# Two attentions on TensorE, VectorE and ScalarE: a rotation placed one step later, and a transposed output placed in another PSUM bank

## The reference, cut to what matters

```python
q, k = rotate(norm(x) @ wq.T + bq), rotate(ctx @ wk.T + bk)   # 16 heads of 8; no biases in layer 3
v = ctx @ wv.T + bv
p = softmax(q @ k.T / sqrt(8))                        # per head, 64 x 64
x = x + tanh(gate) * ((p @ v) @ wo.T + bo)
```

## Time and profile before

| | |
|---|---|
| median of 3 runs | 589.69 us |
| the profiled execution's own time | 589.77 us |
| its span, first to last instruction | 588.0 us |
| TensorE busy | 559.3 us |
| VectorE busy | 441.0 us |
| ScalarE busy | 402.3 us |
| first attention, from its first scores to the projection of its second half | 128.8 to 167.8 us |
| second attention, from and to the same steps | 439.9 to 478.5 us |

### The profile page before, as it was taken

The page is one execution under the profiler, slowest core; times in us unless marked ns, Lnnn a source line. Parts: engine busy times, 40 slices in busy tenths (PEclk is TensorE's granted clock), DMA queues, the critical chain, the costliest instruction groups (busy, mean ns, idle before and its releaser), DMA issues.

```text
span 588.0 us, 8733 instructions
## 1 busy us (share of the span) xinstructions
PE 559.3 (95%) x3258; PEld 387.0 (66%) x3258; DVE 441.0 (75%) x692; ACT 402.3 (68%) x561; POOL 101.9 (17%) x69
## 2 busy tenths in 40 slices
PE   8999999898999999999996999999999999999997
PEld 5688787656767767765331346566546677888886
DVE  3377987868839799987889775766768828787786
ACT  3698899855856755426999865534504858888875
POOL 5400000000210000003999703200000310000000
PEclk8999999999999999999999899999999999999999
DMA  6118120300100369220000024506400100811100
GB/s 242 33 41 310 50 71 1 116 1 2 56 1 2 127 243 230 65 72 1 7 1 1 1 71 117 174 3 175 147 36 3 42 32 3 322 42 67 36 2 36
DMA packets 19342, 43.81 MB, mean 75 GB/s; under 512 B 2090, under 2 KB 7594, under 8 KB 19300
## 3 DMA queue, kind: packets, MB, share of 16 engines
q1 hardware_dynamic: 19300, 43.25, 22.7%
HBM read 42.55 MB, written 0.70 MB: 74 GB/s over the span
## 4 chain that ended last, share of the span: by engine, by line
PE 69%; DVE 15%; ACT 11%; issue 3%; POOL 1%; DVEq 0%; ACTq 0%; POOLq 0%
PE ps L820 36%; ACT work L1219 7%; PE ps L862 4%; PE ps L569 3%; PE ps L552 3%; DVE h_lo L1756 2%; PE ps L846 2%; PE ps L848 2%; PE ps L847 2%; PE ps L686 2%; PE ps L559 2%; PE ps L659 2%; PE ps L887 2%; PE ps L801 2%; DVE h_act L1729 2%
## 5 line engine op out<-in xcount | busy, mean ns | idle before, releaser
L1756 DVE TENSOR_TENSOR h_lo<-h_act,h_hi 128x512 fp32r<-128x512 f32 (+1 forms) x114 | 103.6, 913 | 39.7 <-ACT h_hi L1266 38.9
L820 PE MATMUL ps<-n_hi,w_hi 128*128 128x512 f32 x224 | 86.8, 422 | 2.4 <-DVE h_act L1729 1.2
L1266 ACT CAST h_hi<-h_act 128x1024 fp32r<-128x1024 f32 (+1 forms) x88 | 75.4, 857 | 14.6 <-PE ps L820 12.1
L820 PE MATMUL ps<-n_hi,w_lo 128*128 128x512 f32 x224 | 79.7, 391 | 0.0
L820 PE MATMUL ps<-n_lo,w_hi 128*128 128x512 f32 x224 | 79.6, 390 | 0.0
L1969 POOL TENSOR_TENSOR rstd<-var_eps,minus_half 128x4 f32<-128x4 f32 x16 | 17.2, 1075 | 312.1 <-DVE var_eps L1411 312.1
L1219 ACT ACTIVATE work<-work,p_rest 128x2048 f32<-128x2048 f32 x31 | 59.5, 2000 | 1.0 <-DVE work L1609 1.0
L1259 ACT ACTIVATE h_act<-ps 128x512 f32<-128x512 f32 x44 | 26.3, 598 | 45.6 <-PE ps L820 45.4
L820 PE MATMUL ps<-h_hi,w_hi 128*128 128x512 f32 x162 | 56.2, 395 | 0.1
L820 PE MATMUL ps<-h_hi,w_lo 128*128 128x512 f32 x162 | 55.3, 390 | 0.0
L820 PE MATMUL ps<-h_lo,w_hi 128*128 128x512 f32 x162 | 55.3, 390 | 0.0
(11 more groups left out here) (235 smaller groups left out, 1041.1 us busy)
## 6 DMA issues: line engine op xcount, KB each, us to landing
work<-g_rows SPq DMA_DIRECT2D x36, 512.0 KB, 5.8
w_f<-in_w SPq DMA_DIRECT2D x20, 512.0 KB, 3.7
w_f<-in_w SPq DMA_DIRECT2D x8, 384.0 KB, 3.2
work<-g_rows SPq DMA_DIRECT2D x8, 256.0 KB, 7.3
work<-g_rows SPq DMA_DIRECT2D x4, 384.0 KB, 7.2
diag<-in_w SPq DMA_DIRECT2D x2, 512.0 KB, 4.7
work<-in_w SPq DMA_DIRECT2D x2, 512.0 KB, 4.4
w_f<-in_w_rest SPq DMA_DIRECT2D x2, 384.0 KB, 4.6
```

What stands on the lines that cost most here:

```text
L820: mm = pe.matmul(dst[i], wap(wt, e, lo, size, rows), mv[i], start=(first and c == 0), stop=(last and c == 2))
L1266: act.copy(places(h_hi, m, step), places(h_act, m, step)).then_inc(s["hi"], 1)
L1756: dve.tensor_tensor(lo, src, hi.bitcast(F32), ALU.subtract).then_inc(s["lo"], 1)
```

## The change

Four edits, which act together in both attentions.

- `query_rows(i, 2)` on VectorE is called in step 1 behind output(1) instead of in step 0 behind output(0).
- `query_rows(i, 2)` on ScalarE is called in step 3 behind the exponential of couple 3 instead of in step 2.
- `turn_out(0)` writes the last 128 columns of bank 6 (the values' bank) instead of the first 128 of bank 7, and `out_copy(0)` reads them there. The other couples still use bank 7.
- The waits follow: turn_out(0) waits for the second `ao` of the attention, that is output(1), where it waited for the rotation of the second quarter; turn_out(1) waits for that rotation; values(2) waits also for out_copy(0).

```diff
+        def out_turned(p):
+
+            return ps[:, 7, 0:P] if p else ps[:, 6, HALF - P:]
...
                     if g:
                         pe.wait_ge(at["ao"], g)
+                    if p == 2:
+                        pe.wait_ge(at["aocp"], g - 1)
...
                     if p == 0:
+                        pe.wait_ge(at["ao"], g + 2)
+                    if p == 1:
                         pe.wait_ge(at["qT"], 3 * i + 3)
-                    pe.transpose(ps[:, 7, 0:P], ao[:, p % 2], ident).then_inc(at["aot"], 1)
+                    pe.transpose(out_turned(p), ao[:, p % 2], ident).then_inc(at["aot"], 1)
...
-                        ins = act.activation(aoT[:, p * P:(p + 1) * P], ps[:, 7, 0:P], ACT.Identity, bias=abias[:, 6:7])
+                        ins = act.activation(aoT[:, p * P:(p + 1) * P], out_turned(p), ACT.Identity, bias=abias[:, 6:7])
...
-                    if p in (1, 2):
-                        query_rows(i, p)
+                    if p in (1, 3):
+                        query_rows(i, 1 + p // 2)
...
                     output(p)
-                    if p == 0:
+                    if p == 1:
                         query_rows(i, 2)
```

More of the change, by code:

```diff
@@ L1136, in out_copy @@
                     if i == 0:
-                        ins = act.activation(aoT[:, p * P:(p + 1) * P], ps[:, 7, 0:P], ACT.Identity, bias=abias[:, 6:7])
+                        ins = act.activation(aoT[:, p * P:(p + 1) * P], out_turned(p), ACT.Identity, bias=abias[:, 6:7])
                     else:
-                        ins = act.copy(aoT[:, p * P:(p + 1) * P], ps[:, 7, 0:P])
+                        ins = act.copy(aoT[:, p * P:(p + 1) * P], out_turned(p))
                     ins.then_inc(at["aocp"], 1)
```

## The result

| | before | after |
|---|---|---|
| median, 22 runs each beside one another | 589.03 us | 590.31 us |
| the profiled execution's own time, span | 589.77, 588.0 us | 590.54, 588.8 us |
| ratio, 95% interval | | 1.0024 (1.0015 to 1.0033) |
| values(1) to values(7), first attention, in the trace | 20.69 us | 21.66 us |
| the same, second attention | 20.47 us | 21.61 us |

The account below looks back on a forecast made before the run. TensorE, busy 95% of the span, was taken to bound the kernel. Turn(3)'s lateness of 0.78 + 0.93 gave +1.71 us, a median of 591.4 us (+0.29%), forecast 591.1 to 591.8, range 589.9 to 592.2.

Parts of the forecast that it names:

- Part 1: VectorE, rotation behind out(1): out(1) ends at 145.51 instead of 146.67, its four instructions still taking 2.96 us.
- Part 2: TensorE, turned(0) in bank 6: it waits for out(1), released 0.05 after `ao`, and starts 1.18 us later.
- Part 3: TensorE, values(2): the stall moves in front of scores(4); values(2) starts 0.06 and 0.30 us later in the two attentions.
- Part 4: ScalarE behind turned(0): exp(3) starts late, so turn(3) is late by 0.78 and 0.93 us.
- Part 5: ScalarE's masked copy of the second quarter, behind exp(3): taken as 0, upper end 0.1 us in each attention.
- Part 6: The rotation's new readers: turned(1)'s wait is hidden by 0.8 us, and out(2) ends at 150.03, before values(3) at 150.7.
- The sum: Both attentions together: 0.78 + 0.93 = +1.71 us, passed on whole to the end of the kernel.
- The bound above: Upper limit of the loss, +2.0 us: 1.71, 0.2 for the masked copy, 0.1 for handovers from TensorE to ScalarE.
- the gain: Rival: turned(0) isn't held by its new wait, stalls of 1.05 and 0.80 us go, 587.8 us; chance 8%.
- the "only the first stall" rival: Rival: values(2) is late by 0.06 and 0.30 but exp(3) is not, 590.1 us; 15%, with later slack giving part back.
- The clock: Rival: TensorE's clock falls to half behind its two idles, up to 3.95 us more, 593.5 or 595.4; chance 5%.

Follow-up runs that it names:

- e2: Changed kernel with ScalarE's copy of turned(0) put behind the two copies of turn(2) and the weight cast; ratio 1.0009 to the kernel before.
- e5: e1 with ten bf16 matmuls, read by nothing, put on TensorE ahead of turned(0) in each attention; ratio 1.0094 to the kernel before.
- e3: e2 with turned(0) put behind scores(4) on TensorE instead of in front; ratio 1.0009 to the kernel before.
- e1: Changed kernel with both edits of the rotation taken back, turned(0) still in bank 6 and waiting for out(1); ratio 1.0169 to the kernel before.
- r_before: The kernel before, unchanged, run once more for a second trace and the scatter; ratio 0.9996.
- r_after: The changed kernel itself run once more, for the size of the effect; ratio 1.0040 to the kernel before.
- e4: Kernel before with VectorE's masked copies done by ScalarE and the copy of turned(0) behind turn(2)'s copies and the weight cast; ratio 0.9983.

## Why the prediction was right

The forecast was +1.7 us by two steps, a stall moved in front of scores(4) and exp(3) late behind turned(0). Both are in the trace, and e2 separates them: 1.42 us go with the order on ScalarE and 0.69 stay. In e5, at a full clock, turned(0) comes 1.15 and 0.90 later behind values(1) than in the changed kernel, and the sum is larger by just that (4.16 - 2.11 = 2.05): the loss follows the wait for out(1). e3 takes turned(0) from in front of scores(4) and wins nothing, so the last 0.69 is not one stall's: values(3) then waits for out(2).

- **Part 1** held to 0.01: out(1) ends 2.97 after the maximum over scores(3) begins, and this begins 0.07 after the scores end.
- **Part 2** held: the wait is 1.11 and 1.12 us. Its release is 0.15 after `ao` (144.97 to 145.12), where I had taken 0.05 from values(2).
- **Part 3**: the sign held, the size was off: values(2) is late by 0.25 and 0.45 instead of 0.06 and 0.30. 0.10 is that release. In the first attention 0.07 more is ScalarE's first copy of turn(2), which by the timeline ends at 146.30 (145.72 + 0.58), 0.14 before values(2) starts: values(2) comes 1.09 behind scores(4) there, but 1.03 in the second attention and 1.02 in e2, where that copy is done earlier. I had this copy ending 0.1 before it is needed and left that margin out of the bounds. The rest, 0.02 and 0.05, is small steps that no run separates.
- **Part 4** held and is the larger: turn(3) is late by 0.91 and 1.09 instead of 0.78 and 0.93, by the same 0.10 and small steps. e2 takes it out and leaves 0.69.
- **Part 5** held: the masked copy costs nothing that shows. turn(3) to values(3) is 2.05 instead of 1.99, but these 0.06 lie between turn(3) and scores(5), which wait for no such copy; from scores(5) to values(3) it is 1.02 in both kernels.
- **Part 6** held: out(2) ends at 149.48 and values(3) starts at 150.36. The cover that I named as gone without part 4 is gone in e2: values(3) starts 0.05 behind the end of out(2), at 7.76 behind values(1) instead of 7.52. Of these 0.24, 0.05 are out(2)'s; I had said about 0.1.
- **The sum**: 2.11 in the attentions for 1.71. The bound above, 2.0, was too low by 0.1. Passing the shift on whole held inside the attentions and behind them, and failed between them, where 0.3 to 0.8 came back (last section). The time of 1.0024 is nearer to the forecast of 1.0029 than the trace is (3.6 thousandths), because that return, which I had not foreseen, hides the term that was too small: partly luck. The median of 590.31 lies in the range of 589.9 to 592.2, but under the 591.1 to 591.8 that had 68%: the kernel before was at 589.03 beside it, where I had reckoned from 589.69, its first three times. The ratio on that base makes 591.1.

One reading was weaker than the prediction made it. That values(2) starts right behind `ao` says nothing on bank against address: it overwrites the columns that out(1) reads, and it has a wait for that. In no run does a transpose write bank 6 while VectorE reads it; what the runs show is the cost of the wait as the program has it.

The rivals: the gain did not come, since turned(0) is held by 1.1 us; the "only the first stall" rival is what e2 looks like, and it needed an edit to get there. ScalarE's idle of 0.75 before the change was thin evidence against that rival, since turn(2) ended only at 144.54 of that trace (143.45 + 1.09); the idle of 3.25 after it shows the order plainly. The clock did not fall in the attentions of the changed kernel (1.00 in every 5 us), but e1 shows how near the rival was: with 2.26 and 2.02 us in front of turned(0) instead of 1.11 and 1.12 it costs 4.6 us.

## What to carry to other kernels

A wait that moves forward in an engine's list takes everything behind it along, so price it by the step behind it that others wait for (here exp(3), through ScalarE's copy), not by the stall that it removes. A stall names the first place where a loaded engine shows; before moving the work, follow that engine one couple further, since taking the two masked copies off VectorE (0.40 us each) gave 0.5 us, and 1.5 with ScalarE's order mended, while the best with the rotation in its new place was 0.3, with those copies moved as well. Two orders that look equal for one engine can differ by 0.5 to 0.7 us per attention for the next: an instruction that waits should stand behind those that are ready.

## What the runs showed of the hardware

TensorE's clock fell to half behind idles of 2.26 and 2.02 us in e1, and stayed at 1.00 with idles of 1.11 and 0.50 in the changed kernel. In e1 it was at half for 6.7 us each time. It also dips elsewhere, not in every execution, and that is as large as the effect studied. Windows of the kernel before and, second, of e2:

```profile
10.00:20.00 10.00, 9.42 (x65) 7.31 (x66) 6.85 (x10) 5.44 (x12) 2.82 (x3) 0.83 0.24 96
```

```profile
10.00:20.00 10.00, 9.61 (x74) 7.04 (x74) 6.19 (x9) 5.97 (x13) 3.67 (x3) 1.00 0.23 90
```

Where the first dip is missing, values(1) starts at 140.4 to 140.5 instead of 141.9 to 142.6, some 2 us earlier, and one kernel's times lie in two groups: the changed kernel's 22 are 588.6 to 589.3 at a mean clock of 0.996 to 0.999, or 590.2 to 591.7 at 0.994. A median of few runs is a draw from these.

A second dip lies in layer 2, and its place follows the kernel. It is at 332 to 336 and 331.5 to 335 us in the two traces of before, and begins at 319.5 to 321 and lasts some 4 us in all three of the changed kernel; here r_before and r_after:

```profile
320.00:330.00 10.00, 8.89 (x54) 2.67 (x54) 8.80 (x8) 9.68 (x7) 10.00 (x4) 1.00 0.01 2
330.00:340.00 10.00, 9.20 (x54) 4.47 (x54) 7.02 (x20) 8.60 (x7) 4.52 (x6) 0.83 0.00 0
```

```profile
320.00:330.00 10.00, 9.82 (x53) 2.51 (x45) 7.93 (x7) 8.83 (x7) 9.59 (x3) 0.83 0.01 2
330.00:340.00 10.00, 8.91 (x61) 4.66 (x61) 8.06 (x23) 10.00 (x8) 4.79 (x6) 1.00 0.00 0
```

With it goes the length of the stretch between the attentions, though no instruction there differs: 290.3 and 290.2 us before, 289.5, 289.9 and 289.6 changed. So 0.3 to 0.8 of the 2.11 us comes back there. The timelines say where. The same eight transposes, before and after:

```profile
332.12 2.06 PE L569 MATMUL ps<-p_first,rstd 128*128 128x128 f32 x8
```

```profile
333.33 1.16 PE L573 MATMUL ps<-p_first,rstd 128*128 128x128 f32 x8
```

Before the change they lie in the dip. In the changed kernel the dip is over by then. It fell on matmuls of a stretch in which TensorE waits for ScalarE again and again:

```profile
320.71 3.74 PE L809 MATMUL ps<-work,p_rest 128*32 128x512 f32 x16 [1.13 <-ACT work L1227]
```

The two traces run level until there: an instruction of ScalarE (L1219 before, L1227 after) starts 131.09 and 131.12 us behind the first attention's values(7). A later one (L1280, L1288) starts 181.40 and 180.58 behind it, and this 0.8 stays. (r_after, at 289.9, first loses 0.4 near 210 us; why was not looked into.)

Other kernels fit. e3 has a dip at 314.5 to 317.5 besides the one at 332, and a stretch of 290.3, as before. e4 and its repeat (291.2 both) have one more, 6.7 us long from 285.5 and 287.5 on, and e5 (291.6) one at 291 to 294.5; so e4 loses 0.9 of its 1.49 there. No run moved a dip on purpose, so the cause is read from the traces and not tested by itself; why a dip lies elsewhere in one kernel than in another stays open.
